# A Perceiver block in one launch: the last of 257 keys as a third accumulation step on 128x32 tiles, two small products on column tiles

## The reference

```
x = x + xattn(layernorm(x), ctx)        # 16 heads of 32, softmax over 257 keys
x = x + delta_rule_attention(layernorm(x))
x = x + top2_of_8_experts(layernorm(x))

# cross attention
attn = softmax((q * scale) @ k.T)       # 32 queries x 257 keys per sequence and head
out  = attn @ v                         # then @ proj_w + proj_b
# delta rule, per token
alpha = exp(-exp(A_log) * softplus(x @ Wa.T + dt_bias))
q = q / norm(q) / sqrt(32);  k = k / norm(k)
S = S * alpha;  S = S + k * ((v - k @ S) * beta);  y = q @ S
```

## Time and profile before

| | |
|---|---|
| median of 3 runs | 3275.37 us (3274.96 to 3275.93) |
| span of the profiled execution, first to last instruction | 3280.0 us |
| its own time | the profile gives the span alone; it lies 4.6 us above the median |
| TensorE, matmuls | 3097.4 us busy, 94% |
| VectorE | 2009.3 us, 61% |
| ScalarE | 1337.9 us, 41% |
| GpSimd | 641.3 us, 20% |
| mean granted clock of TensorE | 0.971 |
| first pass / second pass | the second pass starts at about 2590 us |

### The profile page before, as it was taken

How to read it: one execution, slowest core, us unless ns; L and a number is a source line. 1 busy time by engine, 2 the same in 40 slices (tenths; PEclk the granted TensorE clock), 3 DMA queues, 4 the chain that set the end, 5 groups by cost and what they waited for, 6 DMA issues and landing times. The chain is left out here.

```text
span 3280.0 us, 87701 instructions
## 1 busy us (share of the span) xinstructions
PE 3097.4 (94%) x35570; PEld 2267.9 (69%) x35570; DVE 2009.3 (61%) x4107; ACT 1337.9 (41%) x3360; POOL 641.3 (20%) x514
## 2 busy tenths in 40 slices
PE   7999999999999999999999999999999788898984
PEld 5777777777777777777777777777777455544542
DVE  3333367666776677666667766667676477893323
ACT  3444444444444444444444444444443233322321
POOL 0011111111111111111111111111111376601234
PEclk9999999999999999999999999999999888899997
DMA  4222322232222222322232223222321688545479
GB/s 168 69 73 76 105 93 91 86 103 84 81 79 98 85 81 85 98 84 81 79 102 90 81 79 102 84 81 86 108 82 55 170 255 247 166 135 157 145 264 324
DMA packets 297853, 378.10 MB, mean 115 GB/s; under 512 B 159568, under 2 KB 211536, under 8 KB 296016
## 3 DMA queue, kind: packets, MB, share of 16 engines
q1 hardware_dynamic: 287184, 338.19, 32.7%
q0 software_dynamic: 10240, 33.56, 3.0%
HBM read 258.17 MB, written 189.01 MB: 136 GB/s over the span
## 5 line engine op out<-in xcount | busy, mean ns | idle before, releaser
L120 PE MATMUL ring<-cond_high,wkv_high 128*128 128x342 f32 (+1 forms) x1152 | 404.6, 351 | 43.7 <-issue 20.8
L120 PE MATMUL ring<-cond_low,wkv_high 128*128 128x342 f32 (+1 forms) x1152 | 371.4, 322 | 0.0
L120 PE MATMUL ring<-cond_high,wkv_low 128*128 128x342 f32 (+1 forms) x1152 | 370.3, 321 | 0.0
L615 ACT ACTIVATE shared_rows<-ring,kvb 128x342 f32<-128x342 f32 (+1 forms) x384 | 209.6, 546 | 376.6 <-PE ring L120 376.6
L840 DVE TENSOR_REDUCE neg_max<-score 128x4 f32<-128x1028 f32 x128 | 157.3, 1229 | 288.3 <-PE score L952 288.3
L120 PE MATMUL ring<-wkv_high,cond_high 128*128 128x512 f32 x768 | 316.6, 412 | 0.0
L169 DVE TENSOR_TENSOR prod<-coef,deltas 128x64 f32<-128x64 f32 (+30 forms) x248 | 306.8, 1237 | 5.9
L120 PE MATMUL ring<-wkv_high,cond_low 128*128 128x512 f32 x768 | 303.1, 395 | 0.0
L120 PE MATMUL ring<-wkv_low,cond_high 128*128 128x512 f32 x768 | 302.7, 394 | 0.0
L649 ACT ACTIVATE prob<-score,neg_max 128x257 f32<-128x257 f32 x512 | 236.5, 475 | 135.3 <-DVE neg_max L840 135.3
L120 PE MATMUL mix<-experts,xs_t 128*128 x624 | 287.1, 604 | 0.0
(11 more groups left out here) (199 smaller groups left out, 5499.8 us busy)
## 6 DMA issues: line engine op xcount, KB each, us to landing
cond<-cond_t_dram SPq DMA_DIRECT2D x128, 385.5 KB, 4.2
xs<-slot_rows SPq DMA_DIRECT2D x78, 256.0 KB, 2.8
slot_rows<-ys SPq DMA_DIRECT2D x78, 256.0 KB, 2.0
x_rows<-x SPq DMA_DIRECT2D x64, 256.0 KB, 2.7
vb_rows<-vgb SPq DMA_DIRECT2D x64, 256.0 KB, 3.4
x_in<-x_dram SPq DMA_DIRECT2D x32, 256.0 KB, 3.4
kk_rows<-kk_rows_s SPq DMA_DIRECT2D x32, 256.0 KB, 2.7
qk_rows<-decay SPq DMA_DIRECT2D x32, 256.0 KB, 2.8
```

What stands on the lines that cost most here:

```text
L120: last = pe.matmul(out, lhs_t, rhs, start=start and i == 0, stop=stop and i == len(terms) - 1)
L615: act.activation(k_t[:, group, at:at + n], ring_bank[bank][:, 0:n], ACT.Identity, bias=kvb[:, group:group + 1]).then_inc(ring.free[bank], 1)
```

## The change

The last key becomes a third step of the same form as the first two. `v_last` grows to 128 partitions: four DMAs a batch copy the last key's values to the 32 partitions of each step group, the rest stays zero or is masked. `prob_last` is the last column of `prob` times a constant, `own_step`, that is 1 where the partition's token is the column's token; it needs no transpose and no bank. `attend` then has 16 matmuls of 128x32 weights with 32 columns for it. L964 and the four uses of the ring go. The sums of squares and the decay product are done on four column tiles of 32 each: 32 matmuls for 8, and 16 for 4.

```diff
-            "BT", "K22", "K23", "QT", "V2", "V00", "V01", "L0", "V10", "V11", "O0", "L1", "V20", "V21", "O1",
-            "L2", "V30", "V31", "O2", "L3", "GT", "O3"]
+            "BT", "K22", "K23", "QT", "V2", "V00", "V01", "V10", "V11", "O0", "V20", "V21", "O1",
+            "V30", "V31", "O2", "GT", "O3"]
...
-        v_last = sb("v_last_s", [HG, 2, P])
+        v_last = sb("v_last_s", [P, 2, HG, P])
...
-        prob_last_t = sb("prob_last_t", [HG, 4, HG, N])
+        prob_last = sb("prob_last", [P, HG, N])
+        own_step = sb("own_step", [P, N])
...
+                own.did(pool.memset(v_last[:], 0.0))
...
+                dve.tensor_reduce(own_step[:], ident[:].rearrange("p (a n) -> p n a", a=4), AX.X, ALU.add)
...
-                dve.tensor_copy(v_last_all, bank[:]).then_inc(v_last_moved, 1)
+                dve.tensor_copy(v_last_all.rearrange("p (g a e) -> p g a e", g=HG, a=4),
+                                bank[:].rearrange("p (a g e) -> p g a e", a=4, g=HG)).then_inc(v_last_moved, 1)
...
-                sp.dma_start(v_last[:, b % 2, :], v_last_d[bass.ds(u * BU + b, 1), :].rearrange("r (a x) -> (r a) x", a=HG))\
-                    .then_inc(v_last_loaded[b % 2], 16)
+                for g in range(HG):
+                    sp.dma_start(v_last[g * N:g * N + N, b % 2, g, :],
+                                 v_last_d[bass.ds(u * BU + b, 1), g * P:g * P + P].to_broadcast([N, P]))\
+                        .then_inc(v_last_loaded[b % 2], 16)
...
-                    bank = ring.wait_full(dve, f"L{b}", u)
-                    dve.tensor_tensor(prob_last_t[:], ring_bank[bank][0:HG, 0:P].rearrange("p (g t) -> p g t", g=4)
-                                      .unsqueeze(2).to_broadcast([HG, 4, HG, N]),
-                                      ident[0:HG, 0:HG].unsqueeze(1).unsqueeze(3).to_broadcast([HG, 4, HG, N]), ALU.mult)\
-                        .then_inc(ring.free[bank], 1)
+                    dve.tensor_tensor(prob_last[:], prob[:, b % 2, :, M - 1].unsqueeze(2).to_broadcast([P, HG, N]),
+                                      own_step[:].unsqueeze(1).to_broadcast([P, HG, N]), ALU.mult).then_inc(prob_t1_ready, 1)
...
-                bank, full = bank_of(f"L{b}", u)
-                pe.matmul(bank[0:HG, 0:P], prob[:, b % 2, :, M - 1], ident[:], start=True, stop=True).then_inc(full, 1)
...
-                pe.wait_ge(prob_t1_ready, n + 1)
-                pe.wait_ge(v_last_loaded[b % 2], (u * 2 + b // 2) * 16 + 16)
-                if b == BU - 1:
-                    ring.wait_read(pe, f"L{b}", u)
+                pe.wait_ge(prob_t1_ready, 2 * n + 2)
+                pe.wait_ge(v_last_loaded[b % 2], (u * 2 + b // 2) * (16 * HG) + 16 * HG)
...
-                for g in range(HG):
-                    part = slice(g * HD, g * HD + HD)
-                    last = pe.matmul(bank[part, 0:P], v_last[:, b % 2, part],
-                                     prob_last_t[:, g].rearrange("p a t -> p (a t)"), start=False, stop=True)
+                for a in range(HG):
+                    for g in range(HG):
+                        last = pe.matmul(bank[g * HD:g * HD + HD, a * N:a * N + N], v_last[:, b % 2, g, a * HD:a * HD + HD],
+                                         prob_last[:, a, :], start=False, stop=(a == HG - 1))
...
-                        pe.matmul(square_columns[i][:, 4 * g:4 * g + 4], kq_squared[:, i, g * P:g * P + P], head_of[:],
-                                  start=True, stop=True)
+                        for b in range(BU):
+                            pe.matmul(square_columns[i][b * N:b * N + N, 4 * g:4 * g + 4],
+                                      kq_squared[:, i, g * P + b * N:g * P + b * N + N], head_of[:], start=True, stop=True)
...
-                    products(pe, alpha_columns, [(x1n_t[:, c, :], wa[:, c, :]) for c in range(DC)]).then_inc(alpha_ready, 1)
+                    for c in range(DC):
+                        for b in range(BU):
+                            seq = slice(b * N, b * N + N)
+                            ins = pe.matmul(alpha_columns[seq, :], x1n_t[:, c, seq], wa[:, c, :], start=(c == 0),
+                                            stop=(c == DC - 1))
+                    ins.then_inc(alpha_ready, 1)
```

## The result

The changed kernel takes 3298.1 us (median of five runs, 3290.02 to 3305.26); the kernel before, 3275.37 us (five runs, 3273.19 to 3284.43). The ratio is 1.0054, with a 95% interval of 1.0037 to 1.0072: slower by half a per cent, where 3236 us was forecast. The profiled execution is the fastest of the five and has a span of 3288.2 us.

What follows compares the result with a forecast made beforehand. It took TensorE's issued work as the bound, with VectorE's path to q_s a near rival. Terms -64 + 5 - 31 - 6 + 56 = -40 on 3280.0 gave 3240; the median being 4.6 lower, 3236 us, range 3180 to 3259.

Steps and rivals of the forecast that it cites:

- the same: In batches 0 and 1, the last key's passes plus scores take 0.99 us after the change, against 1.02 before.
- no instruction stall: Rival: the next instruction block is prefetched in time, so no new wait appears; 3187 us, chance 0.24.
- +5: Last key in attend (L986): 32 narrow passes replace 8, with extra return cost in batches 2 and 3; +5 us.
- the terms gave 96: Cuts without the stall: -64 last key's transpose, +5 last key in attend, -31 squares, -6 decay product.
- 4-column matmuls might cost what wide ones do: Rival: narrow matmuls cost as much as wide ones, so the squares gain nothing; 3241 us, chance 0.08.
- VectorE, the DMAs of v_last and ScalarE's wait for cond cost nothing: VectorE's saved 49 us, 12 more DMAs a unit and later cond loads were charged as nothing.
- +56: Squares and Gram matmuls: two block boundaries in one burst stall TensorE 1.8 us in each of 31 turns.
- less some 0.2 for the sequencer's lead: In the squares-and-Gram burst, the 2.0 us stall was reduced by 0.2 for the sequencer running ahead, to 1.8.
- any offset from -25 to 140 stalls: In the squares-and-Gram burst, the stall was claimed for any boundary offset in that range, so a miscount of 30 is harmless.
- by the same count no two boundaries are within 4 us there: Attend bursts: boundaries lie too far apart in time, so no instruction stall was charged there.
- slower: Rival: instruction supply stalls in more than one place, 4.9 us a turn against 3.0 gained; 3331 us, chance 0.07.
- The wait for q_s: TensorE's wait for VectorE's q_s (L1055) was to stay near 5 us, a term of 0.

Runs made afterwards that it cites:

- the two runs with one part alone: Changed kernel with squares and decay product as before: 3205.3 us; kernel before with only squares and decay product on column tiles: 3245.9 us.
- the nine runs of the table: Changed kernel with 0, 32, 64, 96, 128, 160, 192, 224 or 256 unused TensorE instructions added ahead of its loop: 3181.4 to 3365.8 us.

## Why the prediction was wrong

**The cuts were real, and larger than forecast.** The last transpose to the second product after it: from the first transpose to that product is 1014.42 - 1013.25 = 1.17 us, before 1016.66 - 1014.99 = 1.67, so 0.50 a batch as worked out. In batch 0 attend and scores take 1013.25 - 1011.64 = 1.61 instead of 1.71: 0.10 better than "the same". From the last product's start to the Grams is 1065.33 - 1064.43 = 0.90, forecast 0.94, before 1.92. The decay product takes 1051.73 - 1051.11 = 0.62 instead of 0.96, forecast 0.60, with some 0.1 of return behind it. The run with 96 instructions more, which has no stall in a burst, comes to 3181.4, where the rival "no instruction stall" said 3187; its turn lasts 76.37 us where 76.4 was forecast without a stall. That this agrees so well is in part luck. From start to start, in the two runs with one part alone, the last key's places gain 2.41 us a turn (forecast 1.85: the term "+5" for the last key in attend is -12, since in each batch the stretch with its 32 passes got about 0.1 shorter instead of staying or growing), the squares 1.03 and the decay product 0.23. That is 3.67 a turn, 117 us, where the terms gave 96; more waiting for q_s and more idle time at the turn's start take 0.44 back. That 4-column matmuls might cost what wide ones do is refuted: 64 of them in 0.65 us. That VectorE, the DMAs of v_last and ScalarE's wait for cond cost nothing held: ScalarE waits 7.8 us for cond in the whole run, 8.2 before, and L859 takes 0.28 us.

**The mechanism was right, its place wrong, its size too small.** What failed is the term "+56" for a new wait for instructions. The forecast had one stall a turn, in the Gram matmuls, 56 us; there are two, in attend, 91.0 us of idle time (117 us from start to start), and none in the Grams. The count of instructions was good: borders at 177 + 256n of a turn, 5 off the forecast's. Two steps behind the term failed.

The first is "less some 0.2 for the sequencer's lead". The border at 433, 13 behind the first square, was crossed in time: in the window 1062.85 to 1062.95 of the changed kernel stands one packet,

```profile
q8 instruction: 1, 0.02, 80.8%
```

1.8 us ahead of the first square (1064.68). The block was asked for while TensorE was still in the slow products before, so the sequencer's lead is far over 0.2 us there. With 2.4 us from packet to use, the block is there near 1065.3, and TensorE needs it near 1066.1. So "any offset from -25 to 140 stalls" holds at 45, 77 and 109 (1.8 to 2.0 us of idle time a turn each, the forecast's 1.8), and not at 13. The forecast also left out what follows a stall there: with 192 more instructions the passes behind it cost another 1.15 us a turn at the lower clock, 3.1 with the 1.94 of the stall from start to start, so with the stall where it was forecast the term would have been near 96 us. The Trainium skill ("TensorE: Matmul & The Clock Gate", Architectural detail: the array is 16× 32×32, not 1× 128×128) gives TensorE a queue 64 deep. That it can run ahead by more than 13 instructions agrees with this; that 45 stall in full does not follow from it, and no run here shows the depth.

The second is "by the same count no two boundaries are within 4 us there". As a count it holds: the border before 1713 (1457) lies 22 instructions ahead of the burst of batch 1 (1479), in products of 0.23 us, so TensorE itself was past it near 1016, and the 234 instructions of the burst up to 1713 are used up by 1020.1. What fails is the conclusion. The packet starts only at 1018.65, 0.16 behind the burst's first matmul, and TensorE goes on at 1021.0. The forecast counted time between borders; what counts is the time from the request. The sequencer's own rows show what lies between: at the head of attend it works through waits (L971 to L974), and they stand behind the border 1457 in the program (two views of one line each, 1013 to 1019; first and last start, us):

```profile
L971 PEldq ALU_OP  x1: 36/36/36, 1014.4 to 1014.4; - x1
...
L974 PEldq EVENT_SEMAPHORE  x1: 51/51/51, 1017.4 to 1017.4; - x1
```

So it was past the border by 1014.4 and the packet came 4.2 us later, but 1.2 us after it had left the last wait. In all 30 turns the packet follows that last wait by 1.1 to 1.4 us. With 32 more instructions the border (1425) lies further ahead, the sequencer leaves the waits 0.8 to 1.6 us sooner, and there too the packet follows by 1.1 to 1.7. Here, then, the request goes with the end of the waits and not with the border; why it does, no run shows. The stall in batch 2 has the same form, with the packet mostly 0.1 to 0.3 us behind the burst's first matmul.

The rival "slower" (0.07) had stalls in more than one place from 3.0 us a turn on: this is what came, though with none in the Grams. Per turn, from start to start: cuts of 3.67, stalls of 3.77, slow passes behind them 0.30, the wait for q_s 0.54 more ((21.9 - 5.1) / 31), "issue" at L120 0.42 less. From the 79.57 us of a turn before this gives 80.09, which is what a turn takes.

**The wait for q_s** did not stay near 5 us, as the step on it had it. It is 21.9 in the changed kernel and 11.4 with 96 more instructions. TensorE's stretch before q_s became shorter than forecast, since the stall moved from that stretch into another. The runs with a stall in the Grams, ahead of q_s, bear this out: they wait 2.4 to 3.3 us for it (160, 192 and 224 more), the other changed ones 11.4 to 21.9.

**The account of the difference between the changed kernel and the one with 96 more.** Medians are 116.7 apart, the profiled spans 111.9. The idle time in the rows counts from the modelled end of a pass, so it is less than what a stall costs. Taken from start to start of the same matmuls, the mean turn is 3.72 us longer: 2.13 at the stall in batch 2, 1.64 at that in batch 1, 0.30 in slower passes behind the former, 0.41 at q_s, 0.79 less at the turn's start, 0.03 elsewhere. Over 30 turns that is 111.7 us; ahead of them and behind them the two executions differ by some 2 us, one way and the other. Nothing of weight is left over.

**What stays open.** Why the request for the next block goes out when it does. A burst without waits at its head and with the same borders was not tried. Nor is it shown how many blocks TensorE holds. In 6 of 30 turns the packet of batch 2 starts 0.7 to 1.9 us late, and what holds it up was not tested. The "issue" row at L120 (28.3 us with 96 more, 7.8 in the changed kernel), most of it at the turn's start, was not followed up.

## What to carry to other kernels

When an edit splits matmuls into more and shorter ones, count the instructions between borders of 256 and the time that the densest 256 take; where that is under the 2.4 us from packet to use, and the packet isn't asked for ahead of the burst, the loop's offset can be worth more than the edit (3181 to 3366 us for one loop body). Before such an edit is judged slower or faster, time it at some offsets, with a few dead instructions ahead of the loop; the kernel before has the same claim to it (moved, it gained 11 us; the best time of the changed one is still 86 us below that). A gain in busy time that does not show in the span asks for the "issue" rows of the waits before any other.

## What the runs showed of the hardware

- An offset of the code by exactly one block of 256 instructions gives the same time but for the added work and nearly the same stalls (3298.1 and 3303.0 us; 91.0 and 97.6); 64 instructions give up to 184 us.
- Where TensorE stops for a block, the next instruction comes 2.2 to 3.4 us after the packet has started, mostly 2.4. The Trainium skill ("Runtime: NRT & Kernel Launch", Instruction fetch mechanics) calls such refills hidden; 59 to 98 us of stalls in bursts of narrow matmuls, in five of the nine runs of the table, speak against it there.
- A loop's branch back seems to fetch too: a turn of the changed kernel has 8 borders and 10 instruction packets. Where a border lies 17 instructions behind the loop's start, TensorE stands idle for up to 5.5 us in a turn.
- After such a stall the granted clock can fall: 0.72 over 6 us and 0.57 over 3 us at 160 instructions more, 0.66 over 4 us at 192, with 512-column passes at 0.85 us from start to start. With 192 more this adds 1.15 us a turn to a stall of 1.94. It happened in 16 to 20 of 30 turns and not in others with the same stall; what decides it was not tested.
